# Local attention in a Trainium2 transformer block: query and key projections grouped ahead of each window's heads, one norm chain for both, and the softmax reciprocal taken before its broadcast

## The chip, the cores and the metric

One Trainium2 chip, all 8 cores; each core runs the same program on its own half of a sequence (4 sequences of 8192 tokens, 4096 tokens a core, with a halo of 1152 tokens recomputed). The metric is device microseconds of the slowest core.

## The reference

Two parts, each with a residual and a layer norm behind it. The first is a linear attention over the whole sequence. The second, `_L0_ffn_ref`, runs two layers, and the change lies in the attention of these two. Cut to what matters:

```python
def _layer(x, ...):                      # DEPTH = 2, HEADS = 8, DIM_HEAD = 64, WINDOW = 512
    h = shift_token(x)                   # upper half of the channels one token later
    q, k, v = jnp.split(h @ wqkv, 3, axis=-1)
    q = l2norm(q) * qs                   # t / max(norm(t), 1e-12), per head
    k = l2norm(k) * ksc
    q, k = rotary_xpos(q, k)
    o = local_attention(q, k, v)         # softmax over this window and the one before, masked
    x = x + o @ wo
    h = layernorm(shift_token(x)) @ w1 + b1
    a, g = jnp.split(h, 2, axis=-1)
    return x + (a * gelu(g)) @ w2 + b2
```

## The kernel before

The stages run one after another: a linear attention (`build_p1`, `build_p2`), then `build_layer(0)`, its MLP, `build_layer(1)`, its MLP, and a final norm. Every stage is written as a list of operations per engine; each engine runs its list in order, and an operation waits on semaphores for the operations named in its dependencies. So the order in which the operations are added is the order of each engine's queue.

The attention of `build_layer` goes over the sequence in windows of 512 tokens, `w` from 0 to 10. Four helpers do the projections of a window:

- `piece_tab` loads the rotary tables of one window by a DMA on the GpSimd queue, as soon as the last user of the tables is done.
- `piece_v` makes the values: 4 tiles of 128 tokens, 8 matmuls each into PSUM bank `P[6]`, and a copy to `vt` (line 943).
- `piece_q(pw, j)` makes the queries of one tile of 128 tokens: 8 matmuls into `P[2]` (line 959), Square on ScalarE (964), a sum per head on VectorE (966), Sqrt on ScalarE (970), max and reciprocal (972, 974), then the scaling that reads `P[2]` (976), the product with `qs_rep` (981) and three rotary operations (983, 987, 992).
- `piece_k(pw, j)` does the same for the keys in the same bank (lines 1004 to 1038). Its matmuls wait for the scaling of the queries at line 976, since that frees `P[2]`.
- `piece_T` transposes the rotated tiles on TensorE (1051, 1065) and copies them on ScalarE into `qf`, `kf_e`, `kf_o`. In the queues it stands ahead of `piece_q` of the next tile.

The attention for key window `pb = w - 1` loops over 8 heads. For each head and each of 4 key tiles, TensorE makes scores (line 1182, masks 1189 and 1193) into the banks 5/3 or 0/1 by turns, ScalarE exponentiates them (1196, 1200), and TensorE multiplies by the values (1138 into `P[6]` for the query window that ends here, called left, and 1145 into `P[7]` for the next one, called right). Line 1206 clears `P[7]` ahead of the second key tile and waits for the last copy out of it (1232). At the end of a head VectorE adds the saved half (1215), clamps the sum of weights (1217), and casts it (1219); TensorE broadcasts the sum over 64 partitions into `P[2]` (1221); VectorE takes the reciprocal of these 64x512 numbers (1225), multiplies (1227), and copies the right half to `O_acc` (1232). The first value product of the next head waits for 1227. After 8 heads the output projection follows (1264, 1268).

Windows 0 and 1 are projected in one piece ahead of the heads. From then on the projection of window `w + 1` is laid between the heads of window `w`: behind each even head one `piece_q`, behind each odd head one `piece_k`, and `piece_T` ahead of the following `piece_q`. The matmuls of `piece_q` and `piece_k` wait for line 1227, as the broadcast and the reciprocal use `P[2]` too. In iteration 9 of each layer there is nothing left to project, so its 8 heads run plain; iteration 10 has only the left half. In layer 1, iteration 1 has only the right half.

## Time and profile before

| | us |
|---|---|
| median of the runs | 11552.49 (2 runs, 11524.73 to 11580.26) |
| the profiled execution | 11389.46 |
| its span, first to last instruction of the slowest core | 11387.9 |
| TensorE busy | 6611.0 |
| VectorE busy | 3372.7 |
| ScalarE busy | 1937.8 |
| attention of layer 0 | about 2893 to 4949 |
| attention of layer 1 | about 7110 to 9094 |

The span runs from the first to the last instruction of the slowest core. A row of the trace gives the start, the duration, the engine, the line and the tiles, and in brackets how long the engine had been idle and what released it. A granted clock of 1.0 is TensorE's full speed, 0.5 the lower of its two levels.

### The profile page before, as it was taken

The page shows a single profiled execution, that of the slowest core. Times are in us where ns is not written, and L with a number is a line of the kernel's source. Part 1 is how long each engine was busy: PE and PEld are TensorE (multiplying, and loading weights), DVE is VectorE, ACT ScalarE, POOL GpSimd, SP SyncE. Part 2 cuts the span into 40 slices and gives each one's busy share as a digit, 9 for nine tenths or more (in the row PEclk, how much of TensorE's full clock was granted, in tenths as well). Part 3 has the DMA queues.
Part 4 walks back from the last instruction along what each step waited for, and adds up shares of the span by engine and source line. Part 5 has one row for each costly group of instructions (what it writes and reads, how often), then busy time and mean ns, then how long its engine had stood idle before and what let it go on. Part 6 is the DMA issues. An engine that isn't in the chain of part 4 may idle for free.

```text
span 11387.9 us, 75913 instructions; the slowest of 8 cores (11360.9 to 11387.9 us)
## 1 busy us (share of the span) xinstructions
PE 6611.0 (58%) x27498; PEld 2682.4 (24%) x27498; DVE 3372.7 (30%) x4692; ACT 1937.8 (17%) x3121; POOL 91.3 (1%) x136
## 2 busy tenths in 40 slices
PE   0488645554455555557687775555555567778821
PEld 0133211112122222223232222222222123222311
DVE  0011133333444444431212211344444410221234
ACT  0001011111132333210001000333233200101000
POOL 1000000000000000000000000000000000000000
PEclk9979877676666665656899987666665567989955
DMA  9501300000100000001122223000000001222221
GB/s 117 60 1 15 39 0 7 8 8 9 19 1 2 1 2 1 0 12 24 53 73 50 63 67 84 3 1 1 2 1 1 2 22 33 59 63 71 60 56 51
DMA packets 610316, 325.47 MB, mean 29 GB/s; under 512 B 489180, under 2 KB 541004, under 8 KB 608416
## 3 DMA queue, kind: packets, MB, share of 16 engines
q0 software_dynamic: 65024, 79.23, 5.7%
q1 hardware_dynamic: 310496, 137.55, 4.6%
q10 hardware_dynamic: 234432, 103.83, 3.6%
q8 instruction: 228, 3.74, 0.1%
q14 instruction: 136, 1.11, 0.0%
HBM read 374.31 MB, written 59.77 MB: 38 GB/s over the span
## 4 chain that ended last, share of the span: by engine, by line
PE 47%; DVE 22%; DMA 10%; ACT 8%; issue 7%; another core or an unknown queue 4%; DVEq 1%; ACTq 0%; POOL 0%; SPq 0%; POOLq 0%
PE M0b L1506 5%; PE M1b L1506 5%; DMA w2b<-w2bf 4%; DMA w1g<-w1bf 4%; PE kps L486 3%; PE vps L497 2%; DVE L0b L1225 2%; DVE L1b L1225 2%; PE M0b L1563 2%; ACT pt L1196 2%; PE p2b L747 2%; PE M1b L1563 2%; PE p2b L653 2%; PE p2b L632 2%
## 5 line engine op out<-in xcount | busy, mean ns | idle before, releaser
L1563 PE MATMUL M0b<-hbuf,w2b 128*128 128x512 bf16 (+1 forms) x1760 | 407.3, 384 | 167.6 <-DMA w2b<-w2bf 115.8
L1506 PE MATMUL M0b<-xt,w1a 128*128 128x512 bf16 (+1 forms) x1760 | 448.0, 403 | 89.2 <-DVE xt L1465 69.1
L486 PE MATMUL kps<-WkSb,X_g 128*128 128x512 bf16 x656 | 204.0, 468 | 426.1 <-DMA WvSb<-Wv 426.1
L1506 PE MATMUL M0b<-xt,w1g 128*128 128x512 bf16 (+1 forms) x1760 | 411.8, 379 | 60.4 <-DMA w1g<-w1bf 59.8
L1539 DVE SCALAR_TENSOR_TENSOR hbuf<-M0b,gout 128x512 bf16<-128x512 f32 x220 | 143.4, 652 | 1000.1 <-ACT gout L1531 988.6
L1506 PE MATMUL M1b<-xt,w1a 128*128 128x512 bf16 x1408 | 388.8, 426 | 76.7 <-DVE xt L1465 56.7
L1563 PE MATMUL M1b<-hbuf,w2b 128*128 128x512 bf16 x1408 | 345.1, 395 | 128.6 <-DMA w2b<-w2bf 86.1
L1539 DVE SCALAR_TENSOR_TENSOR hbuf<-M1b,gout 128x512 bf16<-128x512 f32 x176 | 121.8, 692 | 830.8 <-ACT gout L1531 821.7
L1506 PE MATMUL M1b<-xt,w1g 128*128 128x512 bf16 x1408 | 343.7, 388 | 17.3 <-DMA w1g<-w1bf 14.4
L1138 PE MATMUL L0b<-pt,vt 128*65 128x512 bf16 (+1 forms) x320 | 137.5, 430 | 314.9 <-ACT pt L1200 282.0
L1531 ACT ACTIVATE gout<-M0b 128x512 bf16<-128x512 f32 x220 | 124.4, 565 | 1096.4 <-PE M0b L1522 632.9
L1225 DVE RECIPROCAL L0b<-L0b 64x512 f32<-64x512 f32 x80 | 268.6, 3358 | 63.5 <-PE L0b L1221 63.5
L1138 PE MATMUL L1b<-pt,vt 128*65 128x512 bf16 (+3 forms) x288 | 122.7, 426 | 282.8 <-ACT pt L1200 249.1
L729 PE MATMUL p2tp<-ident_s,gated 128*128 128x128 bf16 x328 | 41.5, 306 | 407.0 <-DVE gated L718 407.0
L1531 ACT ACTIVATE gout<-M1b 128x512 bf16<-128x512 f32 x176 | 105.1, 597 | 935.6 <-PE M1b L1522 477.3
L1563 PEld LDWEIGHTS M0b<-hbuf,w2b 128*128 128x128 bf16 x1760 | 164.2, 104 | 409.9 <-issue 276.2
L632 PE MATMUL p2b<-X_g,WqSb 128*128 128x512 bf16 (+1 forms) x704 | 176.7, 423 | 143.0 <-DVE X_g L804 87.5
L1196 ACT ACT_TABLE_LOAD x130 | 166.8, 1283 | 540.6 <-PE L0b L1193 279.1
L1225 DVE RECIPROCAL L1b<-L1b 64x512 f32<-64x512 f32 x72 | 241.8, 3358 | 57.2 <-PE L1b L1221 57.2
L747 PE MATMUL p2b<-gatedT,WoSb 128*128 128x512 bf16 (+1 forms) x704 | 199.9, 440 | 83.1 <-ACT ao L751 69.3
L1196 ACT ACTIVATE pt<-L0b,mrowH 128x512 bf16<-128x512 f32 (+1 forms) x320 | 213.5, 670 | 198.0 <-PE L0b L1193 104.8
L1196 ACT ACTIVATE pt<-L1b,mrowH 128x512 bf16<-128x512 f32 (+1 forms) x320 | 213.4, 670 | 191.4 <-PE L1b L1193 98.5
(362 smaller groups left out, 10632.5 us busy)
## 6 DMA issues: line engine op xcount, KB each, us to landing
w1a<-w1bf SPq DMA_DIRECT2D x198, 256.0 KB, 3.3
w1g<-w1bf ACTq DMA_DIRECT2D x198, 256.0 KB, 3.4
w2b<-w2bf SPq DMA_DIRECT2D x198, 256.0 KB, 2.6
w2b<-w2bf ACTq DMA_DIRECT2D x198, 256.0 KB, 2.6
w1bf<-w POOLq DMA_DIRECT2D x8, 2816.0 KB, 210.4
outT<-fin_o SPq DMA_DIRECT2D x32, 512.0 KB, 3.5
w2bf<-w POOLq DMA_DIRECT2D x8, 1408.0 KB, 281.4
X_g<-x_extT POOLq DMA_DIRECT2D x4, 2624.0 KB, 43.9
```

The lines of the kernel that those rows point to most:

```text
L486: mm = s.add("tensor", lambda t, c=c, half=half, xs=xsl, st=(c == 0): t.matmul(kps[half][:, :], xs(c), Wk[:, c, 512 * half:512 * (half + 1 ...
L497: mm = s.add("tensor", lambda t, c=c, half=half, xs=xsl, st=(c == 0): t.matmul(vps[half][:, :], xs(c), Wv[:, c, 512 * half:512 * (half + 1 ...
L632: mm = s.add("tensor", lambda t, c=c, fin=fin, pb=pb, g0=g0, Ng=Ng, st=(fin == 0): t.matmul(P[pb][:, 0:Ng], Wq[:, fin, 128 * c:128 * (c + 1)],
L653: mm = s.add("tensor", lambda t, c=c, half=half, pb=pb, tcol=tcol, st=(c == 0): t.matmul(P[pb][:, :], sb["X"][:, c, tcol:tcol + 128], Wh[: ...
L747: mm = s.add("tensor", lambda t, c=c, fin=fin, pb=pb, Ng=Ng, st=(fin == 0): t.matmul(P[pb][:, 0:Ng], Wo[:, fin, 128 * c:128 * (c + 1)], ga ...
L1138: s.add("tensor", lambda t, j=j, h=h, kslot=kslot, n_l=n_l, st=st: t.matmul(P[6][0:65, 128 * j:128 * j + n_l], vt[kslot][:, j, 65 * h:65 * ...
L1196: e1 = s.add("scalar", lambda sc, j=j, kti=kti, qn=qn, bankF=bankF: sc.activation(pt[j % 2][:, 0:min(qn, 512)], bankF[:, 0:min(qn, 512)], ...
L1225: rcp = s.add("vector", lambda v: v.reciprocal(P[2][0:64, 0:512], P[2][0:64, 0:512]), [trp])
L1506: mm = s.add("tensor", lambda t, banks=banks, wt=wt, half=half, fin=fin, nn=nn, st=(fin == 0): t.matmul(banks[half][:, 0:nn], wt[:, fin, : ...
L1531: tg = s.add("scalar", lambda sc, jb=jb, half=half, nn=nn: sc.activation(gout[:, 512 * half:512 * half + nn], P[jb + 2 + half][:, 0:nn], A ...
L1539: th = s.add("vector", lambda v, j=j, jb=jb, half=half, nn=nn: v.scalar_tensor_tensor(h_buf[:, j, 512 * half:512 * half + nn], P[jb + half ...
L1563: mm = s.add("tensor", lambda t, c=c, j=j, sl=sl, half=half, nn=nn, st=(j == 0), sp=(j == 21): t.matmul(P[c][:, 0:nn], w2b[sl][:, 128 * c: ...
```

## The change

Four edits, all in `build_layer`. No projection is laid between heads any more: in every iteration with a window left, its values, queries, keys and transposes are done in one piece ahead of the heads. `piece_q` ends with a copy of the raw queries from PSUM to a bf16 tile, `qraw`, and the rest of its chain moves into `piece_k`, where one Sqrt, one max and one reciprocal serve both sums (16 numbers a token). And the reciprocal of the softmax sum is taken on one row of 512 numbers ahead of the cast and the broadcast, in place of on 64x512 behind it.

```diff
             def piece_q(pw, j):
...
                 t_qrd = rd
-                sq = s.add("scalar", lambda sc: sc.activation(
-                    bnf[:, 8:16], bnf[:, 0:8], AF.Sqrt), [rd])
...
-                t1 = s.add("vector", lambda v: v.tensor_tensor(
-                    ubuf[:, :], P[2][:, :],
-                    bass.AP(bnf, 8, [[24, 128], [1, 8], [0, 64]]),
-                    ALU.mult), [rc])
-                t_uq = t1
...
-                return s.add("vector", lambda v: v.tensor_add(
-                    qrot[:, :], qrot[:, :], ubuf[:, :]), [tb])
+                tqr = s.add("vector", lambda v: v.tensor_copy(
+                    qraw[:, :], P[2][:, :]), [rd])
+                t_uq = tqr
...
             def piece_k(pw, j):
...
-                    bnf[:, 16:24], xqk[:, :].rearrange("p (h d) -> p h d", d=64),
+                    bnf[:, 8:16], xqk[:, :].rearrange("p (h d) -> p h d", d=64),
                     AX.X, ALU.add), [tks])
                 sq = s.add("scalar", lambda sc: sc.activation(
-                    bnf[:, 16:24], bnf[:, 16:24], AF.Sqrt), [rd])
+                    bnf[:, 16:32], bnf[:, 0:16], AF.Sqrt), [rd])
...
+                t1 = s.add("vector", lambda v: v.tensor_tensor(
+                    ubuf[:, :], qraw[:, :],
+                    bass.AP(bnf, 16, [[32, 128], [1, 8], [0, 64]]),
+                    ALU.mult), [rc])
+                t2 = s.add("vector", lambda v: v.tensor_mul(
+                    qhat[:, :], ubuf[:, :], qs_rep[:, :]), [t1, t_w8])
...
+                tq = s.add("vector", lambda v: v.tensor_add(
+                    qrot[:, :], qrot[:, :], ubuf[:, :]), [tb])
                 t1 = s.add("vector", lambda v: v.tensor_tensor(
                     ubuf[:, :], P[2][:, :],
-                    bass.AP(bnf, 16, [[24, 128], [1, 8], [0, 64]]),
-                    ALU.mult), [rc])
+                    bass.AP(bnf, 24, [[32, 128], [1, 8], [0, 64]]),
+                    ALU.mult), [tq])
...
-                return tk
+                return tq, tk
...
-                if w < n_proj and w <= CL:
+                if w < n_proj:
                     piece_tab(w)
                     piece_v(w)
                     pend = None
                     for j in range(4):
                         if pend is not None:
                             piece_T(w, pend[0], pend[1], pend[2])
-                        tqt = piece_q(w, j)
-                        tkt = piece_k(w, j)
+                        piece_q(w, j)
+                        tqt, tkt = piece_k(w, j)
                         pend = (j, tqt, tkt)
                     piece_T(w, pend[0], pend[1], pend[2])
-                elif w < n_proj:
-                    piece_v(w)
...
+                            trc = s.add("vector", lambda v: v.reciprocal(
+                                tsum[64:65, :], tsum[64:65, :]), [tmx])
                             tcb = s.add("vector", lambda v: v.tensor_copy(
-                                rrowb[0:1, :], tsum[64:65, :]), [tmx])
+                                rrowb[0:1, :], tsum[64:65, :]), [trc])
                             trp = s.add("tensor", lambda t: t.matmul(
                                 P[2][0:64, 0:512], sb["ones_row"][0:1, 0:64], rrowb[0:1, :],
                                 start=True, stop=True), [tcb, t_tt1, t_uq, t_uk])
-                            rcp = s.add("vector", lambda v: v.reciprocal(
-                                P[2][0:64, 0:512], P[2][0:64, 0:512]), [trp])
                             to2 = s.add("vector", lambda v, h=h, B=B_left: v.tensor_tensor(
-                                tsum[0:64, :], P[2][0:64, :], ALU.mult), [rcp, t_wo2])
+                                tsum[0:64, :], P[2][0:64, :], ALU.mult), [trp, t_wo2])
...
-                        if il:
-                            ph = h
-                            jj = ph // 2
-                            if ph % 2 == 0:
...
-                                self._tq_il = piece_q(pw, jj)
-                            else:
-                                tkt = piece_k(pw, jj)
-                                pend_il = (jj, self._tq_il, tkt)
-                    if il:
-                        piece_T(pw, pend_il[0], pend_il[1], pend_il[2])
```

## Rows read from the trace of the kernel before

**Rows 1.** The page, busy time, share of the span and instructions by engine.
```profile
PE 6611.0 (58%) x27498; PEld 2682.4 (24%) x27498; DVE 3372.7 (30%) x4692; ACT 1937.8 (17%) x3121; POOL 91.3 (1%) x136
```

**Rows 2.** Windows: stretch, length, busy by engine, granted clock, DMA share, GB/s.
```profile
2976.05:3251.07 275.02, 143.56 (x488) 61.12 (x488) 122.05 (x189) 79.70 (x136) 1.48 (x2) 0.64 0.02 2
3251.07:4705.66 1454.59, 775.71 (x2744) 323.51 (x2744) 631.29 (x870) 466.49 (x756) 4.44 (x6) 0.61 0.01 1
4705.66:4853.48 147.82, 74.27 (x300) 31.87 (x300) 58.75 (x61) 36.74 (x69) 0.00 (x0) 0.60 0.00 0
2984.55:3064.26 79.71, 37.90 (x125) 16.70 (x123) 34.12 (x68) 18.38 (x37) 0.74 (x1) 0.68 0.03 4
4714.16:4723.35 9.19, 4.07 (x30) 2.12 (x29) 2.21 (x4) 5.29 (x9) 0.00 (x0) 0.99 0.01 2
7197.42:7396.85 199.43, 113.41 (x416) 52.81 (x416) 72.10 (x141) 79.69 (x136) 1.48 (x2) 0.67 0.02 3
7274.40:7396.85 122.45, 75.56 (x296) 36.30 (x296) 37.41 (x73) 66.71 (x108) 0.74 (x1) 0.62 0.03 4
7396.85:8851.94 1455.09, 777.10 (x2744) 324.28 (x2744) 631.30 (x869) 466.81 (x756) 4.45 (x6) 0.61 0.01 1
8851.94:8998.80 146.86, 73.07 (x300) 31.11 (x300) 58.94 (x62) 36.74 (x69) 0.00 (x0) 0.64 0.00 0
```

**Rows 3.** Groups by line on ScalarE: the table loads.
```profile
L1196 ACT ACT_TABLE_LOAD x130 | 166.8, 1283 | 540.6 <-PE L0b L1193 279.1 <-PE L1b L1193 259.5
L970 ACT ACT_TABLE_LOAD x65 | 83.4, 1283 | 57.3 <-DVE bnf L966 57.3
L1016 ACT ACT_TABLE_LOAD x64 | 82.1, 1283 | 55.7 <-DVE bnf L1012 55.7
```

**Rows 4.** Timeline, projections of window 0, layer 0 (start, us, engine, line, operation).
```profile
2904.44 1.89 PE L939 MATMUL L0b<-wqkv_l,X_g 128*128 128x512 bf16 x8 [0.95 <-DVE vt L943]
...
2942.64 0.69 DVE L966 TENSOR_REDUCE bnf<-xqk 128x8 f32<-128x512 bf16 x1 [5.23 <-ACT xqk L964]
...
2944.31 0.69 DVE L976 TENSOR_TENSOR ubuf<-L0b,bnf 128x512 bf16<-128x512 f32 x1
2945.10 0.42 DVE L981 TENSOR_TENSOR qhat<-ubuf,qsr 128x512 bf16<-128x512 bf16 x1
2945.15 3.39 PE L1004 MATMUL L0b<-wqkv_l,X_g 128*128 128x512 bf16 x8 [3.31 <-DVE ubuf L976]
...
2947.03 0.69 DVE L992 TENSOR_TENSOR qrot<-qrot,ubuf 128x512 f32<-128x512 f32 x1
...
2959.68 0.69 DVE L966 TENSOR_REDUCE bnf<-xqk 128x8 f32<-128x512 bf16 x1 [5.26 <-ACT xqk L964]
```

**Rows 5.** Timeline, one plain head of iteration 9, layer 0.
```profile
4805.44 0.69 DVE L1215 TENSOR_TENSOR tsum<-L0b,Oacc 65x512 f32<-65x512 f32 x1 [6.74 <-PE L0b L1145]
...
4807.31 0.60 PE L1221 MATMUL L0b<-rrowb,ones_row_g 1*64 1x512 bf16 x1 [2.05 <-DVE rrowb L1219]
...
4808.02 3.36 DVE L1225 RECIPROCAL L0b<-L0b 64x512 f32<-64x512 f32 x1 [0.85 <-PE L0b L1221]
...
4809.65 0.37 ACT L1200 ACTIVATE pt<-L0b,mrowH 128x128 bf16<-128x128 f32 x1
4811.48 0.68 DVE L1227 TENSOR_TENSOR osb<-tsum,L0b 64x512 bf16<-64x512 f32 x1
4812.26 0.69 DVE L1232 CAST Oacc<-L0b 65x512 bf16<-65x512 f32 x1
...
4813.10 0.60 PE L1206 MATMUL L0b<-zrow_g,ones_row_g 1*65 1x512 bf16 x1 [4.32 <-DVE Oacc L1232]
...
4814.35 0.63 PE L1138 MATMUL L0b<-pt,vt 128*65 128x512 bf16 x1
...
4819.69 0.69 DVE L1215 TENSOR_TENSOR tsum<-L0b,Oacc 65x512 f32<-65x512 f32 x1 [6.74 <-PE L0b L1145]
```

**Rows 6.** One line's instructions: the reciprocal of the earlier stage, min/median/max ns.
```profile
L786 DVE RECIPROCAL rowB<-rowB x11: 941/3341/3341, 1507.9 to 2837.0; 1x512 f32<-1x512 f32 x10, 1x128 f32<-1x128 f32 x1
```

More of the change, by code:

```diff
@@ L851, in build_layer @@
             xqk = self.sbuf(f"xqk{l}", (128, 512), BF16, es)
-            bnf = self.sbuf(f"bnf{l}", (128, 24), F32, es)
+            qraw = self.sbuf(f"qraw{l}", (128, 512), BF16, es)
+            bnf = self.sbuf(f"bnf{l}", (128, 32), F32, es)
             P = [self.psum(f"L{l}b{i}", (128, 512), F32, es) for i in range(8)]
@@ L969, in piece_q @@
                 t_qrd = rd
-                sq = s.add("scalar", lambda sc: sc.activation(
-                    bnf[:, 8:16], bnf[:, 0:8], AF.Sqrt), [rd])
-                mx = s.add("vector", lambda v: v.tensor_scalar(
-                    bnf[:, 8:16], bnf[:, 8:16], 1e-12, None, ALU.max), [sq])
-                rc = s.add("vector", lambda v: v.reciprocal(
-                    bnf[:, 8:16], bnf[:, 8:16]), [mx])
-                t1 = s.add("vector", lambda v: v.tensor_tensor(
-                    ubuf[:, :], P[2][:, :],
-                    bass.AP(bnf, 8, [[24, 128], [1, 8], [0, 64]]),
-                    ALU.mult), [rc])
-                t_uq = t1
-                t2 = s.add("vector", lambda v: v.tensor_mul(
-                    qhat[:, :], ubuf[:, :], qs_rep[:, :]), [t1, t_w8])
-                ta = s.add("vector", lambda v, j=j: v.tensor_tensor(
-                    ubuf[:, :], qhat[:, :],
-                    bass.AP(tabs, 256 * j + 0 * DF, [[4 * 4 * DF, 128], [0, 8], [1, DF]]),
-                    ALU.mult), [t2, t_tab])
-                tb = s.add("vector", lambda v, j=j: v.tensor_tensor(
-                    qrot[:, :].rearrange("p (h t x) -> p h t x", h=8, t=2),
-                    bass.AP(qhat, 32, [[512, 128], [64, 8], [-32, 2], [1, 32]]),
-                    bass.AP(tabs, 256 * j + 1 * DF, [[4 * 4 * DF, 128], [0, 8], [32, 2], [1, 32]]),
-                    ALU.mult), [ta, self.t_ttq])
-                return s.add("vector", lambda v: v.tensor_add(
-                    qrot[:, :], qrot[:, :], ubuf[:, :]), [tb])
+                tqr = s.add("vector", lambda v: v.tensor_copy(
+                    qraw[:, :], P[2][:, :]), [rd])
+                t_uq = tqr
             def piece_k(pw, j):
@@ L1016, in piece_k @@
                 sq = s.add("scalar", lambda sc: sc.activation(
-                    bnf[:, 16:24], bnf[:, 16:24], AF.Sqrt), [rd])
+                    bnf[:, 16:32], bnf[:, 0:16], AF.Sqrt), [rd])
                 mx = s.add("vector", lambda v: v.tensor_scalar(
-                    bnf[:, 16:24], bnf[:, 16:24], 1e-12, None, ALU.max), [sq])
+                    bnf[:, 16:32], bnf[:, 16:32], 1e-12, None, ALU.max), [sq])
                 rc = s.add("vector", lambda v: v.reciprocal(
-                    bnf[:, 16:24], bnf[:, 16:24]), [mx])
+                    bnf[:, 16:32], bnf[:, 16:32]), [mx])
+                t1 = s.add("vector", lambda v: v.tensor_tensor(
[4 more added lines that the diff above has]
+                    qhat[:, :], ubuf[:, :], qs_rep[:, :]), [t1, t_w8])
+                ta = s.add("vector", lambda v, j=j: v.tensor_tensor(
+                    ubuf[:, :], qhat[:, :],
+                    bass.AP(tabs, 256 * j + 0 * DF, [[4 * 4 * DF, 128], [0, 8], [1, DF]]),
+                    ALU.mult), [t2, t_tab])
+                tb = s.add("vector", lambda v, j=j: v.tensor_tensor(
+                    qrot[:, :].rearrange("p (h t x) -> p h t x", h=8, t=2),
+                    bass.AP(qhat, 32, [[512, 128], [64, 8], [-32, 2], [1, 32]]),
+                    bass.AP(tabs, 256 * j + 1 * DF, [[4 * 4 * DF, 128], [0, 8], [32, 2], [1, 32]]),
+                    ALU.mult), [ta, self.t_ttq])
+                tq = s.add("vector", lambda v: v.tensor_add(
+                    qrot[:, :], qrot[:, :], ubuf[:, :]), [tb])
                 t1 = s.add("vector", lambda v: v.tensor_tensor(
                     ubuf[:, :], P[2][:, :],
-                    bass.AP(bnf, 16, [[24, 128], [1, 8], [0, 64]]),
-                    ALU.mult), [rc])
+                    bass.AP(bnf, 24, [[32, 128], [1, 8], [0, 64]]),
+                    ALU.mult), [tq])
                 t_uk = t1
```

9 lines of the change are left out of this document (removed).

## The prediction

> **What bounds the kernel now.** I read the page first. TensorE is busy 58% of the span, VectorE 30%, ScalarE 17% [rows 1]: no engine is the bound, so a sum of busy times says little and chains of waits decide. The change touches only the attention of the two layers, so I cut that stage into its iterations, from the first value copy of one window to that of the next, with the windows view [rows 2], and read the timeline of one tile of projections [rows 4] and of one plain head [rows 5].
>
> The three kinds of work that the new kernel is built from all exist in this trace. Iterations 2 to 8 of layer 0, heads with projections laid between them, take 1454.59 us, so 207.8 each; layer 1 the same, 1455.09 or 207.9 [rows 2]. Iteration 9, with values, 8 plain heads and the output projection, takes 147.8 in layer 0 and 146.9 in layer 1 [rows 2] (its end is put where the next window's first value copy would have come, after the output projection). And windows 0 and 1 show a projection in one piece. Laying the projections between the heads so costs 207.8 - 147.8 = 60 us a window; in one piece they will have to cost less than that to gain.
>
> **Part 1: projections in one piece.** From the last value copy of iteration 1 to the first reciprocal of its heads there are 79.71 us; in iteration 9, without projections, the same distance is 9.19 [rows 2]. So the old form in one piece costs 79.7 - 9.2 = 70.5 us, more than the 60 it costs between the heads. The reason is in the timeline: a tile pair goes round in 2959.68 - 2942.64 = 17.04 us [rows 4], four make 68.2, and nothing else runs in it, whereas between heads the vector chain of a projection lies beside the scores and exponentials of the next head.
>
> **Part 2: the joined norm chain.** Removed from the way to the keys' matmuls: from the start of the queries' sum to the start of those matmuls there are 2945.15 - 2942.64 = 2.51 us [rows 4]. New: the sum 0.69 and 0.10 of spacing, the copy from PSUM, for which I take 0.69 like every 128x512 operation that reads PSUM here, and 0.15 to TensorE: 1.63. Saved 0.88. But the five query operations, which today run while TensorE makes the keys, now stand between the joint reciprocal and the scaling of the keys, on VectorE, and the keys' transposes and the next tile's matmuls wait behind them. From the start of the queries' scaling to the start of its last add there are 2947.03 - 2944.31 = 2.72 us, with 0.69 + 0.10 for the add itself: 3.51 [rows 4]. The scaling now reads bf16 from SBUF and f32 norms. Bounds are 0.69, as from PSUM, and 0.42, as the all-bf16 product behind it [rows 4]; one operand stays f32, so I take 0.69; the other end would give back 0.27. Sqrt, max and reciprocal of 16 numbers in place of 8 cost nothing visible, and the second set that is saved lay on the part already counted. Net per pair: 3.51 - 0.88 = +2.63, so 19.7 us, and +10.5 for four. The queries' transposes stay hidden: they are ready 3.5 us ahead of the keys'. In windows 0 and 1 this is a plain loss.
>
> **Part 3: table loads.** There are 130 + 65 + 64 = 259 loads of 1.283 us in the attention [rows 3]. After it there are one for Sqrt and one for Exp per window, 36 in all (windows 1 to 9 need one for Exp; 0 and 2 to 9 one for Sqrt): 223 fewer, 286 us of ScalarE. This is no term of its own: the plain head already has none of them, and 147.8 holds its one Exp load. The Sqrt load at a window's start lies on the chain: +1.3 for windows 2 to 9.
>
> The Trainium skill, "ScalarE: Activation LUTs", section "Table sets: the hidden batching unit", says to group activations by table set, which is what this change does and speaks for a gain; it prices a switch at about 2.7 us. The trace shows 1.283 for the load. What the rule would do here is the third rival below.
>
> **Part 4: the reciprocal ahead of the broadcast.** The one-row form exists in the trace: 3.341 us for 1x512 [rows 6], against 3.36 for 64x512 [rows 5]. So it costs the same; only its place changes. Today it runs behind the broadcast, and TensorE makes the next head's first scores beside it; afterwards TensorE waits for it. The head's chain is sum (4805.44), clamp, cast, broadcast (4807.31), reciprocal (4808.02), product (4811.48), copy (4812.26), clear of the bank (4813.10), and 6.59 us more to the next head's sum [rows 5]: 14.25. With the reciprocal ahead, each link stays, so the clear stands 7.66 us behind the sum as before. The first scores and their exponential now start behind the later broadcast. Today the last exponential of them ends 4809.65 + 0.37 - 4807.31 = 2.71 us behind the broadcast, and the first value product stands 4814.35 - 4813.10 = 1.25 behind the clear [rows 5]. In the new order the clear comes 0.71 + 0.68 + 0.10 + 0.84 = 2.33 behind the broadcast, the value product 3.58: it is later than 2.71 by 0.87. So a plain head still takes 14.25, and the cover that was lost was not needed. Only in iteration 10, without copy and clear, the value product could start 1.5 behind the broadcast and must wait for the exponential: 0 to 1.2 a head, taken as 0.6, for 16 heads 10 us, 5 a layer. The table DMA of each window is issued during the heads before and costs nothing; uncovered it would delay the first rotary product.
>
> **The sum, layer 0.** Inserting projections costs 70.5 + 10.5 = 81.0, with a Sqrt load 82.3. Window 0: +10.5. Iteration 1: 147.8 + 81.0 - 275.0 = -46.2, as the projection of window 2 leaves it. Iterations 2 to 8: 7 x (147.8 + 82.3) - 1454.6 = +156.1. Iteration 9: +82.3. Iteration 10: +5. Total +208.
>
> **Layer 1.** Window 0: +10.5. Iteration 1 has no left half, so a plain head there needs the 6.59 and 0.84 from copy to clear, 7.43; eight and some 4 us around them are 63.5 in place of 122.45 [rows 2]: -59.0, with the pairs -48.5. Iterations 2 to 8: 7 x (146.9 + 82.3) - 1455.1 = +149.3. Iteration 9 +82.3, iteration 10 +5. Total +199.
>
> Together +406 us. On the profiled execution, 11389.5, that is 11796; on the median of the runs, 163 us higher for reasons that its profile can't show, 11959, or 3.5% more. The predicted time goes by the median, rounded to 11950.
>
> **The rivals.**
>
> *The clock rises.* The clock in the projections is 0.68 and in the plain windows 0.60 to 0.64 [rows 2]; eight matmuls take 3.39 us where they take 1.89 at full clock [rows 4]. In the new order TensorE's idle time inside a tile pair shrinks between queries and keys (3.31 to about 2.4) and a head's matmuls stand closer together. If the keys' matmuls ran at full clock, 80 x 1.50 = 120 us come back; for the heads, the two plain windows differ by 0.96 us for 0.04 of clock, so some 9 us a window up to full clock, 18 windows: 165. Then +406 - 285 = +121, 11673 by the median: within 2%. Against it: TensorE's wait behind the key matmuls grows by the 3.5 us of the query chain, and the one in front of the broadcast from 2.05 to 5.4 [rows 5], and the key matmuls behind 3.31 us of idle time are slow today [rows 4]. The Trainium skill, "TensorE: Matmul & The Clock Gate", section "Loop structure matters more than you think", warns that waits between bursts of matmuls drop the clock; the trace agrees in those rows, and the rule speaks against this change. Chance 12%.
>
> *The lost cover matters.* If the next head's first scores and exponential came out exposed behind the later broadcast, up to 2.2 us a head (2.71 less the 0.5 of the broadcast itself) for 144 heads would add 317: 12276. The margin is 0.87 us, so this decides once they take 0.9 us longer than now. Chance 5%.
>
> *The table loads were the price.* If the laying-between cost only its loads, and all else stayed hidden as now, 286 us would come back: 11266, faster by 2.5%. It decides if the one-piece projection takes under about 60 - 286 / 16 = 42 us a window. The 70.5 us of the serial form speak against it: the vector chain and not the load fills them. Chance 3%.
>
> **How the numbers follow.** My forecast has 80%, and the range of 8 in 10 is its own: 11740 (half of the clock's 285 us comes back and the median falls by half of its 163 us towards the profiled execution) to 12070 (the sum by the median with 110 us of exposed chain or of slower matmuls). The clock's rival in full lies below it, the lost cover in full above, and so does the loads' rival, below. About 2% is what a measurement tells from no change here. Slower by over 2%: forecast and lost cover, 85%, of which one is moved to within 2% for a clock between the two, so 84%. Within 2%: 13%. Faster: 3%.
>
> **What the profile of the changed kernel would show.** Value copies of iterations 2 to 9 about 230 us apart. A tile pair every 19.7 us. Plain heads every 13.7 to 14.3 us, with TensorE idle 5.4 in front of the broadcast. A one-row reciprocal of 3.34. 36 table loads in the attention. The MLP unchanged. The prediction is wrong if pairs take under 17 us, heads under 12 or over 15, or if the MLP's clock moves with the attention's.

## The result

The changed kernel is slower. Its median is 11940.5 us (11743.6 to 12076.3, 11 runs) against 11534.5 us of the kernel before (11353.6 to 11628.2, 10 runs). The medians count all runs; the ratio, 1.0323 with a 95% interval of 1.0218 to 1.0428, is taken over the fast ones alone, those in which no die ran longer than the other at a lower clock. The forecast was 11950. One execution was profiled; it took 11837.0 us on its slowest core, and its span is 11835.4.

Nearly all the time went where the argument put it, into the attention: 392 us, where the medians are 406 apart. I measure a layer's attention from the first to the last instruction that uses its PSUM banks, and take the median of the eight cores of the one profiled execution:

| us | before | after | difference |
|---|---|---|---|
| attention, layer 0 | 2072.0 | 2275.4 | +203.4 |
| attention, layer 1 | 1999.8 | 2188.6 | +188.8 |
| both | 4071.8 | 4464.0 | +392.2 |
| both MLPs | 3925.9 | 3926.5 | +0.6 |

The predicted +406 stands against +392. The same two stages are the measure of all the experiments below.

The page of the changed kernel, busy time by engine. Against [rows 1] ScalarE has lost 288 us, nearly all of it loads, and the span has grown all the same.

```profile
PE 6689.1 (57%) x27498; PEld 2689.5 (23%) x27498; DVE 3400.4 (29%) x4612; ACT 1649.9 (14%) x2817; POOL 91.5 (1%) x136
```

The windows view of the changed kernel: stretch, length, busy time of TensorE, its weight loads, VectorE, ScalarE and GpSimd, granted clock, DMA share, GB/s. The first two rows are the two attentions of this core, the next two iteration 1 and iterations 2 to 7 of layer 0, then the same of layer 1, and last the MLP of layer 1.

```profile
2821.22:5092.26 2271.04, 1076.10 (x3792) 445.59 (x3792) 929.51 (x1214) 473.54 (x867) 6.69 (x9) 0.60 0.01 1
7236.40:9429.78 2193.38, 1055.02 (x3720) 440.03 (x3720) 879.70 (x1166) 474.44 (x868) 6.70 (x9) 0.59 0.01 1
2929.37:3154.72 225.35, 107.20 (x392) 45.23 (x392) 91.51 (x120) 47.55 (x89) 0.74 (x1) 0.62 0.01 1
3154.72:4529.38 1374.66, 659.35 (x2352) 275.82 (x2352) 549.39 (x722) 292.79 (x540) 4.45 (x6) 0.60 0.01 2
7348.27:7496.05 147.78, 84.57 (x320) 38.67 (x320) 41.66 (x73) 46.78 (x89) 0.74 (x1) 0.57 0.02 2
7496.05:8871.91 1375.86, 662.34 (x2352) 276.61 (x2352) 549.38 (x722) 293.01 (x540) 4.45 (x6) 0.59 0.01 2
9430.00:11328.07 1898.07, 1457.09 (x5520) 533.77 (x5520) 328.01 (x412) 142.51 (x198) 1.06 (x2) 0.76 0.19 49
```

Six iterations take 1374.66 us in layer 0, 229.1 each, and 1375.86 or 229.3 in layer 1, where before took 207.8 and 207.9 [rows 2]. Iteration 1 shows both signs at once: in layer 0 it fell from 275.02 to 225.35, since the projection of window 2 has moved out of it into iteration 2. That time comes back at the other end: iteration 9, which had no projection before, now has one. The last row is a warning about reading a single execution: MLP 1 takes 1898.07 us at a granted clock of 0.76 here, and 1785.56 at 0.85 in the profile of before. Only cores 4 and 5 show it; the six others take 1789 to 1819, and the median of the MLPs has not moved.

The groups by line on ScalarE, the table loads of the changed attention (sum of us, mean ns, idle time before them): 35 in place of the 259 of [rows 3].

```profile
L1186 ACT ACT_TABLE_LOAD x18 | 23.1, 1283 | 20.3 <-PE L0b L1183 10.2 <-PE L1b L1183 10.2
L996 ACT ACT_TABLE_LOAD x17 | 21.8, 1283 | 14.7 <-DVE bnf L992 14.7
```

The timeline of the changed kernel, one tile pair of projections and one plain head (start, us, engine, line, operation, idle time before it and what ended that), which answer to [rows 4] and [rows 5].

```profile
4090.41 0.69 DVE L1002 TENSOR_TENSOR ubuf<-qraw,bnf 128x512 bf16<-128x512 bf16 x1
...
4093.92 0.69 DVE L1019 TENSOR_TENSOR ubuf<-L0b,bnf 128x512 bf16<-128x512 f32 x1
...
4104.45 3.11 PE L984 MATMUL L0b<-wqkv_l,X_g 128*128 128x512 bf16 x8 [2.42 <-DVE qraw L971]
...
4110.15 0.69 DVE L1002 TENSOR_TENSOR ubuf<-qraw,bnf 128x512 bf16<-128x512 bf16 x1
...
4237.01 0.69 DVE L1205 TENSOR_TENSOR tsum<-L0b,Oacc 65x512 f32<-65x512 f32 x1 [6.25 <-PE L0b L1135]
...
4238.32 3.35 DVE L1209 RECIPROCAL tsum<-tsum 1x512 f32<-1x512 f32 x1
...
4242.33 0.60 PE L1213 MATMUL L0b<-rrowb,ones_row_g 1*64 1x512 bf16 x1 [5.50 <-DVE rrowb L1211]
...
4244.66 0.60 PE L1196 MATMUL L0b<-zrow_g,ones_row_g 1*65 1x512 bf16 x1 [0.87 <-DVE Oacc L1222]
...
4244.67 0.37 ACT L1190 ACTIVATE pt<-L0b,mrowH 128x128 bf16<-128x128 f32 x1
...
4245.92 0.63 PE L1128 MATMUL L0b<-pt,vt 128*65 128x512 bf16 x1
...
4250.71 0.69 DVE L1205 TENSOR_TENSOR tsum<-L0b,Oacc 65x512 f32<-65x512 f32 x1 [6.20 <-PE L0b L1135]
```

A pair goes round in 4110.15 - 4090.41 = 19.74 us, where before took 17.04 [rows 4]. The queries' five operations stand where the forecast put them: the keys' scaling starts at 4093.92, 3.51 behind the queries'. In the head, the reciprocal now ends before the broadcast, TensorE waits 5.50 us for it where it waited 2.05 [rows 5], and yet the period is 4250.71 - 4237.01 = 13.70, no longer than before.

### The profile page after: what moved, and what is told of

Same layout as the page of the kernel before. It is cut to its first block, busy times and chain, and to the rows that moved or that the text cites. A ratio compares the mean times of both kernels' runs of the same rounds, so it can differ in the third digit from the quotient of the medians.

```text
span 11835.4 us, 75712 instructions; the slowest of 8 cores (11752.8 to 11835.4 us)
## 1 busy us (share of the span) xinstructions
PE 6689.1 (57%) x27498; PEld 2689.5 (23%) x27498; DVE 3400.4 (29%) x4612; ACT 1649.9 (14%) x2817; POOL 91.5 (1%) x136
## 4 chain that ended last, share of the span: by engine, by line
PE 48%; DVE 26%; DMA 9%; issue 6%; ACT 6%; another core or an unknown queue 4%; DVEq 1%; ACTq 0%; POOL 0%; SPq 0%; POOLq 0%
PE M1b L1482 6%; PE M0b L1482 6%; DVE tsum L1209 4%; DMA w2b<-w2bf 4%; DMA w1g<-w1bf 3%; PE kps L486 3%; PE vps L497 2%; PE M0b L1539 2%; PE M1b L1539 2%; PE p2b L747 2%; PE p2b L653 2%; PE p2b L632 1%; PE L0b L1240 1%; PE L1b L1240 1%
## 5 line engine op out<-in xcount | busy, mean ns | idle before, releaser
L1209 DVE RECIPROCAL tsum<-tsum 1x512 f32<-1x512 f32 x152 | 508.3, 3344 | 16.0 <-DVE tsum L1207 0.5
L1482 PE MATMUL M1b<-xt,w1a 128*128 128x512 bf16 x1408 | 434.6, 465 | 77.0 <-DVE xt L1441 56.6
L1539 PE MATMUL M1b<-hbuf,w2b 128*128 128x512 bf16 x1408 | 390.1, 436 | 112.7 <-DMA w2b<-w2bf 71.4
L1482 PE MATMUL M1b<-xt,w1g 128*128 128x512 bf16 x1408 | 376.0, 416 | 8.5 <-DMA w1g<-w1bf 8.2
L1213 PE MATMUL L0b<-rrowb,ones_row_g 1*64 1x512 bf16 x80 | 48.0, 600 | 440.7 <-DVE rrowb L1211 440.7
L1213 PE MATMUL L1b<-rrowb,ones_row_g 1*64 1x512 bf16 x72 | 43.2, 600 | 396.7 <-DVE rrowb L1211 396.7
L1482 PEld LDWEIGHTS M0b<-xt,w1a 128*128 128x128 bf16 x1760 | 160.5, 104 | 322.9 <-issue 206.7
```

Of the source, the lines that this page charges most:

```text
L1209: trc = s.add("vector", lambda v: v.reciprocal(tsum[64:65, :], tsum[64:65, :]), [tmx])
L1482: mm = s.add("tensor", lambda t, banks=banks, wt=wt, half=half, fin=fin, nn=nn, st=(fin == 0): t.matmul(banks[half][:, 0:nn], wt[:, fin, : ...
L1539: mm = s.add("tensor", lambda t, c=c, j=j, sl=sl, half=half, nn=nn, st=(j == 0), sp=(j == 21): t.matmul(P[c][:, 0:nn], w2b[sl][:, 128 * c: ...
```

## The experiments

My theory: laying the projections between the heads was cheap because the vector chain lay beside other work; done in one piece it stands alone, and the joined chain makes the piece longer, since the queries' operations now stand in front of the keys'. The rivals: one piece alone is no loss worth the name, or all of it; the lost cover of the reciprocal costs time; the table loads were the real price. The first three kernels each take one edit of the change alone, on the kernel before, and the fourth one that is not in the change; the next two start from the changed kernel, and the last two put together what was gained. All attention times below are those of one profiled execution each.

**Placement alone.** The projections go in one piece; the two chains and the reciprocal stay as in before.

```diff
-                if w < n_proj and w <= CL:
+                if w < n_proj:
...
-                elif w < n_proj:
-                    piece_v(w)
...
-                    il = (CL < pw < n_proj)
+                    il = False
```

> Only the first edit: all projections in one piece ahead of the heads, with the old norm chains and the old reciprocal. The two attention stages take 2072 + 2000 = 4072 us before and 2271 + 2193 = 4464 after. Theory A (the loss has two parts: projections that no longer lie beside the heads' work, and the queries' rotary chain that came onto the path): this edit alone gives 16 windows about +11 us each and the small corrections of the first iterations, +186 in the two stages, tile pairs every 17.0 us, plain heads every 13.7 to 14.3 us; about 1.6% in the total. Rival B (the placement is the whole loss, and the joined chain costs nothing): +390 here.

Measured: attention 2173.1 + 2100.3 = 4273.4, +201.6. The ratio is 1.0118 (1.0076 to 1.016). So placement carries half of the loss. A pair took 17.66 us on the mean of 60: the first of a window, with the Sqrt load in it, 18.43, and the others 17.28, near the 17.04 of [rows 4]. This kernel has the loads nearly all taken away too, 18 + 17 are left, and loses all the same.

**The joined chain alone.** `piece_q` and `piece_k` as in the change, but called between the heads as before.

```diff
-                                self._tq_il = piece_q(pw, jj)
+                                piece_q(pw, jj)
                             else:
-                                tkt = piece_k(pw, jj)
-                                pend_il = (jj, self._tq_il, tkt)
+                                tqt, tkt = piece_k(pw, jj)
+                                pend_il = (jj, tqt, tkt)
```

> Only the second edit: queries and keys share Sqrt, maximum and reciprocal, and the raw queries are copied out of PSUM, but the projections stay laid between the heads. Theory A: behind a head with a query projection the exponentials no longer queue behind a reduction, two table loads and a Sqrt on ScalarE, so these head periods fall from 20.8 to about 17.1 us; the periods with a key projection stay near 21, since VectorE has some 3 us to spare before the next head's sum; windows 0 and 1 lose 10.5 us each in both layers; together about -190 us in the two attention stages (1.6% faster). Rival B: the five query operations that moved behind the keys fill VectorE in front of the head's sum, the key periods grow by 3.5 us, and the sum is within 20 us of no change.

Measured: 1970.8 + 1893.2 = 3864.0, -207.8; the ratio is 0.98 (0.9749 to 0.9852). The same edit that makes the changed kernel slower makes this one faster. The timeline of this kernel, one head with queries beside it and one with keys:

```profile
3076.15 0.60 ACT L965 ACTIVATE xqk<-L0b 128x512 bf16<-128x512 f32 x1 [3.77 <-PE L0b L960]
...
3076.90 0.69 ACT L1193 ACTIVATE pt<-L0b,mrowH 128x512 bf16<-128x512 f32 x1 [0.15 <-PE L0b L1190]
...
3084.56 3.36 DVE L1222 RECIPROCAL L0b<-L0b 64x512 f32<-64x512 f32 x1 [0.85 <-PE L0b L1218]
...
3102.38 0.69 DVE L1035 TENSOR_TENSOR krot<-krot,ubuf 128x512 f32<-128x512 f32 x1
...
3102.99 0.68 DVE L1212 TENSOR_TENSOR tsum<-L0b,Oacc 65x512 f32<-65x512 f32 x1
...
3105.56 3.36 DVE L1222 RECIPROCAL L0b<-L0b 64x512 f32<-64x512 f32 x1 [0.85 <-PE L0b L1218]
```

Behind the squares of the queries the exponential starts at once (3076.90): no load, no Sqrt. A head with queries then takes 16.36 us on the mean (15.5 to 17.2), where it took 20.8 before. A head with keys takes 21.0 (3105.56 - 3084.56): it has both loads, and VectorE works through both chains, so that the last add of the keys (3102.38) ends just as the next head's sum starts (3102.99). Four heads with queries save 17.9 us a window; the heads with keys give back 0.7 of it, and the stretch from one window's last head to the next one's first, 64.15 us for 62.14, another 2.0. That is some 15 us for each of 16 windows, 243; windows 0 and 1 of both layers, in one piece, give back 42 at the forecast's 10.5 a window, which leaves 201.

**The reciprocal first, alone.**

```diff
+                            trc = s.add("vector", lambda v: v.reciprocal(
+                                tsum[64:65, :], tsum[64:65, :]), [tmx])
                             tcb = s.add("vector", lambda v: v.tensor_copy(
-                                rrowb[0:1, :], tsum[64:65, :]), [tmx])
+                                rrowb[0:1, :], tsum[64:65, :]), [trc])
...
-                            rcp = s.add("vector", lambda v: v.reciprocal(
-                                P[2][0:64, 0:512], P[2][0:64, 0:512]), [trp])
```

> Only the last edit: the reciprocal on one row ahead of the cast and the broadcast. Theory A (it only changes place in an unbroken chain): head periods as before, 20.6 to 21.1 with projections between and 13.7 to 14.3 plain, iteration 10 from 9.4 to 10.1 us a head, so about +12 us in the two attention stages. Rival (TensorE now stands idle through it, so the next head's scores come late or its clock falls): plain heads over 15 us, or over +60 in the stages.

Measured, in a single run: 2114.3 + 2034.3 = 4148.6, +76.8. This is a miss: the rival's bound of +60 was passed, but with the plain heads unchanged, so not for its reason. The place is plain in the timeline. First the kernel before, a head between projections:

```profile
3104.89 0.37 PE L1221 MATMUL L0b<-rrowb,ones_row_g 1*64 1x512 bf16 x1 [1.98 <-DVE rrowb L1219]
3105.19 1.11 PE L1051 MATMUL L0b<-identF_g,qrot 128*128 128x128 f32 x4
3107.11 1.09 PE L1065 MATMUL L0b<-identF_g,krot 128*128 128x128 f32 x4 [0.82 <-ACT qf L1055]
3109.65 3.57 PE L959 MATMUL L0b<-wqkv_l,X_g 128*128 128x512 bf16 x8 [1.45 <-DVE osb L1227]
```

Then the same head with the reciprocal first:

```profile
3090.96 0.60 PE L1223 MATMUL L0b<-rrowb,ones_row_g 1*64 1x512 bf16 x1 [5.43 <-DVE rrowb L1221]
3091.49 1.12 PE L1051 MATMUL L0b<-identF_g,qrot 128*128 128x128 f32 x4
3093.43 1.09 PE L1065 MATMUL L0b<-identF_g,krot 128*128 128x128 f32 x4 [0.82 <-ACT qf L1055]
3094.31 3.62 PE L959 MATMUL L0b<-wqkv_l,X_g 128*128 128x512 bf16 x8
```

In before, the transposes of the previous tile lie beside the reciprocal of 3.36 us, and the next queries start 3109.65 - 3104.89 = 4.76 behind the broadcast, waiting for the product alone. With the reciprocal first, the broadcast comes 5.43 - 1.98 = 3.45 later, and the queries stand 3.35 behind it, because now the transposes hold them up: 3.45 + 3.35 - 4.76 = +2.04. The heads that carry transposes went from 20.8 to 22.8 us on the mean; there are three of them a window in 16 windows, 48 x 2.0 = 96. The 16 heads of iteration 10 add 12, and the stretch from one window's heads to the next's got 2.3 us shorter (59.80 for 62.14), which gives 16 x 2.3 = 37 back: 71 in all. The plain heads of iteration 9 didn't move, as forecast. So the reciprocal did cover something, only not in the plain heads where I had looked.

**The norm without Sqrt, in place.** Before, with the norm's factor as exp(-0.5 ln(max(sum, 1e-24))) in both chains in place of Sqrt, max and reciprocal. Nothing is moved.

```diff
-                sq = s.add("scalar", lambda sc: sc.activation(
-                    bnf[:, 8:16], bnf[:, 0:8], AF.Sqrt), [rd])
                 mx = s.add("vector", lambda v: v.tensor_scalar(
-                    bnf[:, 8:16], bnf[:, 8:16], 1e-12, None, ALU.max), [sq])
-                rc = s.add("vector", lambda v: v.reciprocal(
-                    bnf[:, 8:16], bnf[:, 8:16]), [mx])
+                    bnf[:, 8:16], bnf[:, 0:8], 1e-24, None, ALU.max), [rd])
+                sq = s.add("scalar", lambda sc: sc.activation(
+                    bnf[:, 8:16], bnf[:, 8:16], AF.Ln), [mx])
+                rc = s.add("scalar", lambda sc: sc.activation(
+                    bnf[:, 8:16], bnf[:, 8:16], AF.Exp, scale=-0.5), [sq])
```

> The kernel before, with 1/norm made as exp(-0.5 ln(max(sum, 1e-24))) on ScalarE, in place of Sqrt, maximum and reciprocal, so that the table set need not change between the heads if one set serves both functions. If the 256 loads between heads vanish: theory A, whose price for laying projections between heads is the reduction, the two loads and the Sqrt that the next head's exponentials queue behind, expects 2.6 us off each of 128 head periods less 0.3 for the second function: 20.8 to about 18.4, some -290 us in the two attention stages. Rival (the loads lie beside other work): under -60 us. If the loads stay, the run only shows one more short function per chain, about +30 us.

Measured: 1917.2 + 1830.2 = 3747.4, -324.4; the ratio is 0.9688 (0.961 to 0.9766). ScalarE's queue between two heads in the kernel before:

```profile
3113.32 0.60 ACT L964 ACTIVATE xqk<-L0b 128x512 bf16<-128x512 f32 x1 [3.78 <-PE L0b L959]
3114.78 1.28 ACT L970 ACT_TABLE_LOAD   x1 [0.87 <-DVE bnf L966]
3116.08 0.21 ACT L970 ACTIVATE bnf<-bnf 128x8 f32<-128x8 f32 x1
3116.30 1.28 ACT L1196 ACT_TABLE_LOAD   x1
3117.60 0.69 ACT L1196 ACTIVATE pt<-L0b,mrowH 128x512 bf16<-128x512 f32 x1
```

and in this kernel:

```profile
3082.88 0.60 ACT L964 ACTIVATE xqk<-L0b 128x512 bf16<-128x512 f32 x1 [3.90 <-PE L0b L959]
3084.92 0.21 ACT L972 ACTIVATE bnf<-bnf 128x8 f32<-128x8 f32 x1 [1.44 <-DVE bnf L970]
3085.22 0.21 ACT L974 ACTIVATE bnf<-bnf 128x8 f32<-128x8 f32 x1
3085.33 0.67 ACT L1196 ACTIVATE pt<-L0b,mrowH 128x512 bf16<-128x512 f32 x1
```

From the squares to the head's first exponential there are 3117.60 - 3113.32 = 4.28 us before and 3085.33 - 3082.88 = 2.45 here. Both loads of each projection are gone, two are left in the attention of both layers, and a head between projections takes 18.5 us on the mean (17.5 to 19.2) in place of 20.8. The 257 loads that went have 257 x 1.283 = 330 us, and 324 us came back. The edit also moved the reciprocal of the norm from VectorE to ScalarE, but that is 0.20 us against 0.21: the loads lay on the path, nearly all of them. The Trainium skill, "ScalarE: Activation LUTs", section "Table sets: the hidden batching unit", names one set that holds both Exp and Ln; the trace agrees, with 2 loads left of 259.

**The changed kernel with the old reciprocal.** `trc` goes out and `rcp` back behind the broadcast; the other edits stay.

```diff
-                            trc = s.add("vector", lambda v: v.reciprocal(
-                                tsum[64:65, :], tsum[64:65, :]), [tmx])
...
+                            rcp = s.add("vector", lambda v: v.reciprocal(
+                                P[2][0:64, 0:512], P[2][0:64, 0:512]), [trp])
```

> The changed kernel with the reciprocal back behind the broadcast, on 64x512. The changed kernel takes 4464 us in the two attention stages. The same edit made in the kernel before cost +77 there, because the reciprocal had covered the transposes of the projection. Theory A: with no projection between the heads there is nothing but the next head's first scores to cover, which has room, so here it is worth only iteration 10, 16 heads at 10.15 in place of 9.4 us: -12 us. Rival C (the cost is the longer idle time in front of the broadcast and comes anywhere): -60 us or more.

Measured, in a single run: 2270.6 + 2188.6 = 4459.2, 4.8 less than the changed kernel, which is within what its cores differ by (2263.3 to 2274.2 in layer 0). A plain head takes 13.87 on the mean against 13.92, a head of iteration 10 9.44 against 10.20. With the first two experiments this splits the +392.2 along a chain of kernels: placement +201.6, the joined chain on top of it +185.8, the reciprocal on top of both +4.8.

**The changed kernel with the transposes later.** In one piece, tile j's query matmuls now go ahead of the transposes of tile j - 1; they wait for `t_uk`, the last reader of their bank, as well.

```diff
                     for j in range(4):
+                        piece_q(w, j)
                         if pend is not None:
                             piece_T(w, pend[0], pend[1], pend[2])
-                        piece_q(w, j)
                         tqt, tkt = piece_k(w, j)
```

> The changed kernel with the transposes of tile j-1 placed between the query and the key matmuls of tile j, in place of ahead of both; the query matmuls then wait for the keys' scaling, the last reader of their bank. Theory A (the tile pair is one chain, and the keys' product, rotary operations and transposes lie on it only through TensorE's order): the 3.8 us between the end of that scaling and the next query matmuls shrink to 0.15, so pairs fall from 19.5 to about 16, for 60 pairs some -205 us in the two attention stages. Rival D (VectorE's own queue, which still has the keys' four operations in front of the next sum, or the transposes in front of the key matmuls, sets the pair): under -60 us.

Measured: 2149.7 + 2053.9 = 4203.6, 260.4 less than the changed kernel, by moving one line. Against before the ratio is 1.0106 (1.0068 to 1.0143): it gives back two thirds of the loss. The timeline of a tile pair:

```profile
2938.89 0.69 DVE L1019 TENSOR_TENSOR ubuf<-L0b,bnf 128x512 bf16<-128x512 f32 x1
...
2939.73 3.27 PE L960 MATMUL L0b<-wqkv_l,X_g 128*128 128x512 bf16 x8 [6.94 <-DVE ubuf L1019]
...
2942.84 0.60 PE L1048 MATMUL L0b<-identF_g,qrot 128*128 128x128 f32 x4
...
2944.32 0.63 PE L1062 MATMUL L0b<-identF_g,krot 128*128 128x128 f32 x4 [0.88 <-ACT qf L1052]
...
2945.42 1.89 PE L984 MATMUL L0b<-wqkv_l,X_g 128*128 128x512 bf16 x8 [0.48 <-DVE qraw L971]
```

The next queries' matmuls wait for the keys' scaling and no longer for the keys' rotation, addition and transposes. The transposes fall into the gap before the key matmuls; TensorE's idle time there shrinks from 2.42 us to 0.48, and in this pair those eight matmuls take 1.89 us, at a granted clock of 1.00, where they took 3.11 at 0.58. That is not so in every pair: of the 60 groups with transposes in front 36 take 1.89, the others 3.04 to 3.48. The rows of the key matmuls of layer 0 in the kernel with placement alone (core 3, as records are missing on its slowest), the changed kernel and this one (sum of us for 40 groups, mean ns of one matmul, idle time before them):

```profile
L1004 PE MATMUL L0b<-wqkv_l,X_g 128*128 128x512 bf16 x320 | 136.3, 604 | 143.2 <-DVE ubuf L976 143.2
L984 PE MATMUL L0b<-wqkv_l,X_g 128*128 128x512 bf16 x320 | 117.8, 534 | 96.9 <-DVE qraw L971 96.9
L984 PE MATMUL L0b<-wqkv_l,X_g 128*128 128x512 bf16 x320 | 106.7, 494 | 31.8 <-DVE qraw L971 31.8
```

Over both layers a group takes 3.41, 2.94 and 2.59 us, so the faster matmuls give 80 x 0.35 = 28 of this kernel's 260 us. Pairs take 15.9 us on the mean (14.5 to 17.8) in place of 19.8. So what made the piece of the changed kernel dear was mostly the order in which TensorE waited for the vector chain, not the amount of work in it. But the piece in its best order is still the dearer place: this kernel's attention is 131.8 us longer than before.

**What was gained, put together.** The joined chain between the heads, Ln and Exp for its norm, and the later transposes in windows 0 and 1.

```diff
-                    bnf[:, 16:32], bnf[:, 0:16], AF.Sqrt), [rd])
+                    bnf[:, 16:32], bnf[:, 16:32], AF.Ln), [mx])
+                rc = s.add("scalar", lambda sc: sc.activation(
+                    bnf[:, 16:32], bnf[:, 16:32], AF.Exp, scale=-0.5), [sq])
...
+                        piece_q(w, j)
                         if pend is not None:
                             piece_T(w, pend[0], pend[1], pend[2])
-                        piece_q(w, j)
```

> The kernel before with projections laid between the heads, plus the joined chain of the change, the ln and exp form of the norm, and the later transposes in windows 0 and 1. Theory A: what each gave alone adds up as far as it takes away the same queue in front of the exponentials: periods with a query projection 16.2, with a key projection about 18.8, so pairs of heads 35.0 in place of 41.6 before, 37.1 with ln and exp alone and 37.3 with the joined chain alone; about -440 us in the two attention stages (to 3630), 3.8% faster than before. Rival E: with both, VectorE's 3.5 us of query operations no longer fit in front of the next head's sum in the shorter key period, which stays at 20 or more: -330 or less.

Measured: 1890.8 + 1805.0 = 3695.8, -376.0 to before; the ratio is 0.9667 (0.9588 to 0.9746). That is 64 us less gain than I had expected. Heads with queries take 16.2 us on the mean (15.6 to 16.9), as forecast, heads with keys 19.6 (19.1 to 20.1) where 18.8 was forecast, and the timeline shows why:

```profile
3206.36 3.36 DVE L1222 RECIPROCAL L0b<-L0b 64x512 f32<-64x512 f32 x1 [0.62 <-PE L0b L1218]
...
3210.66 3.41 PE L984 MATMUL L0b<-wqkv_l,X_g 128*128 128x512 bf16 x8 [4.40 <-DVE osb L1224]
...
3214.22 0.60 ACT L989 ACTIVATE xqk<-L0b 128x512 bf16<-128x512 f32 x1 [10.89 <-PE L0b L984]
```

The key matmuls wait 4.40 us for the product behind the reciprocal, since broadcast and projection share a bank. So all that comes behind the keys starts late: VectorE gets the squares' sum only then, and both chains of the pair run into the next head's sum.

**A bank of its own for the broadcast.** The last kernel with broadcast, reciprocal and product in `P[4]`, which the transposes use, so that the projection's matmuls need not wait for the product. The transposes wait for it instead, and stand behind the query matmuls.

```diff
-                        deps = [t_uk, t_uq, t_tt1]
+                        deps = [t_uk, t_uq]
...
-                                P[2][0:64, 0:512], sb["ones_row"][0:1, 0:64], rrowb[0:1, :],
+                                P[4][0:64, 0:512], sb["ones_row"][0:1, 0:64], rrowb[0:1, :],
...
                             if ph % 2 == 0:
+                                piece_q(pw, jj)
                                 if pend_il is not None:
                                     piece_T(pw, pend_il[0], pend_il[1], pend_il[2])
                                     pend_il = None
-                                piece_q(pw, jj)
```

> The same with the broadcast and the reciprocal in the transposes' bank, so that the projection's matmuls no longer wait for the head's reciprocal and product, and with the transposes behind the query matmuls. Theory A (the reciprocal stands in the chain of the projection's bank): the matmuls, 3.4 us, run beside the reciprocal, and periods without transposes fall by about 2.8 us; those with transposes, which now wait for the product, fall by about 1: some -230 us against the run before it in the two attention stages. Rival F: Square, sum and norm still stand in front of the exponentials in ScalarE's queue and the sum now waits for the reciprocal on VectorE, so nothing is gained: within 40 us.

Measured: 1769.0 + 1709.7 = 3478.7, 217.1 less than the kernel before it and 593 less than before. The median is 10848.0 us, the ratio 0.9476 (0.9417 to 0.9535): faster than both kernels of this case. Its timeline, the start of the keys and the end of that head:

```profile
3300.17 0.60 PE L1218 MATMUL L0b<-rrowb,ones_row_g 1*64 1x512 bf16 x1 [1.98 <-DVE rrowb L1216]
...
3300.70 3.59 PE L984 MATMUL L0b<-wqkv_l,X_g 128*128 128x512 bf16 x8
...
3300.88 3.36 DVE L1222 RECIPROCAL L0b<-L0b 64x512 f32<-64x512 f32 x1 [0.85 <-PE L0b L1218]
...
3313.50 0.69 DVE L1035 TENSOR_TENSOR krot<-krot,ubuf 128x512 f32<-128x512 f32 x1
...
3314.11 0.68 DVE L1212 TENSOR_TENSOR tsum<-L0b,Oacc 65x512 f32<-65x512 f32 x1
```

The key matmuls start 0.53 us behind the broadcast and run beside the reciprocal. A head with keys takes 15.9 us on the mean (15.6 to 16.2) in place of 19.6, and the first of a window, with queries and nothing to transpose, 13.2 (12.4 to 14.3) in place of 16.2. A head with queries and transposes takes 17.0 (16.6 to 17.8) in place of 16.3: it was to fall by 1 us and rose by 0.75, since its transposes now wait for the product. So the total came out near its forecast, -217 for -230, by two misses that offset each other: the key heads fell by 3.7 and not by 2.8. The keys' last add (3313.50) still ends as the next sum starts (3314.11), so VectorE's order may be the next thing in the way of a head with keys; no run tries it.

## Why the prediction was right

The step that decided was **part 1**, the comparison of two figures that were both in the trace: 60 us for laying a projection between heads and 70.5 for one in one piece. Placement alone came out at +201.6 where I had expected +186: the decision and its size held. It holds even for the piece in its best order, which still costs +131.8.

**Part 2** was mis-sized by little. The pair was forecast at 19.7 and is 19.83 on the mean of 60 (18.1 to 21.8); that the two agree so well is luck in part, as the pair that it started from was put 0.6 too low and what was added to it 0.46 too high. The 3.51 us between the two scalings, and the 0.69 for the scaling from `qraw`, came out as taken. But on top of the one-piece kernel the joined chain cost +185.8, where 2.63 x 4 x 20 windows make 210: the pairs that it replaced took 17.66 on the mean and not 17.04, so that 2.17 a pair was added, and 2.17 x 80 = 174 (counted from the keys' sums, 17.20 and 19.88, it was 2.68). What the part left out is the key matmuls: it took them as unchanged, and eight of them fell from 3.41 us to 2.94, by 0.47, the size of what is missing between 2.63 and 2.17. What the part did not tell is that 2.63 is the price of one order of TensorE's queue. With the next queries ahead of the transposes the pair falls to 15.9, below that of before.

**Part 3** held: 35 loads against 36 forecast, and apart from the 1.3 for the Sqrt load at each window's start the loads were no term of the sum. That the old price of the laying-between held its loads in full was not seen: -324.4 without them in place. The third rival was right that the loads were a price (they cost 324 us, more than the 286 it had) and wrong that this change could collect it. A table load taken away between heads shortens the path; the same load taken away by moving the projection out is paid for by the chain that then stands alone.

**Part 4** held for the kernel it was made for. The last exponential ends 4244.67 + 0.37 - 4242.33 = 2.71 behind the broadcast and the value product starts 4245.92 - 4242.33 = 3.59 behind it, so 0.88 against the 0.87 forecast. Plain heads take 13.9 us in both kernels. A head of iteration 10 grew from 9.45 to 10.20, by 0.75 and not 0.6, 12 us for 16 heads against 10 in the sum; in all, the edit costs 4.8. The text said that the cover was not needed; that is so only because edit 1 had taken the transposes away from behind the broadcast. In the old placement the cover was needed, and the edit alone costs 76.8.

**The sum.** By stage, +203.4 and +188.8 stand against +208 and +199. By edit, +201.6, +185.8 and +4.8 stand against +186, +210 and +10, so the total is closer than its parts: an excess of 16 and shortfalls of 24 and 5 offset each other. Iterations 2 to 7 take 229.1 and 229.3 us against 230.1 and 229.2; iteration 1 takes 225.35 against 147.8 + 81.0 = 228.8, and in layer 1 147.78 against 150.9, because a head without a left half takes 6.93 and not 7.43. The step from the profiled execution to the median was the weaker one: 163 us were added for what the profile can't show, and the profiled execution of the changed kernel took 11837.0 where the sum said 11796. Of those 41, -14 are the attention, +112 MLP 1 on the slowest core, and -56 lie ahead of the attention, which starts at 2821 and not at 2877: two differences between executions, the first of them on two cores only and the second ahead of everything that was changed, which happened to offset each other in part. That 11950 lies 10 us from the median is therefore luck; what the argument can claim is the size of the loss, 392 in the stages for a forecast of 406.

**The rivals.** Over the two attentions the clock did not rise: 0.60 and 0.59, against 0.62 and 0.61 before. But in the key matmuls, where this rival put its first term, it did in part: they took 2.94 us a group against 3.41 with placement alone, behind 2.42 us of idle time and not 3.31, so 80 x 0.47 = 38 of its 120 us came back. The heads gave nothing back: plain ones kept their 13.9 us. With the transposes moved into the gap another 28 us came, and that kernel's total of +132, near the +121 worked out for this rival, is chance: most of its 260 us are a wait that went, not a faster clock. The lost cover decided nothing in this kernel (13.9 and 13.9).

**What stays open.** Why the medians of the kernel before differ between chips and sets of runs (11534, 11429, 11436) was not tried; the ratios of the experiments are against runs of the kernel before on the same chip. The last two kernels were not taken apart further: the joining of the chain is not priced separately from the Ln and Exp, and in the last one the new bank not from the transposes behind the query matmuls. Why the key matmuls run faster in some pairs than in others was not tried either.

## What to carry to other kernels

Before grouping work to save set-up costs, price both places from the trace: what the piece costs between the other work, and what it costs standing alone, where its serial chain is all there is. A small edit has no price of its own: the joined chain is worth -208 us between heads and +186 in one piece, and the reciprocal first +77 and +5, so measure or forecast each edit in the placement that it will have. And in an in-order queue ask of each wait whether anything behind it could go first: one call moved ahead of the transposes was worth 260 us, and a bank of its own for the broadcast, together with such a move, 217.

## What the runs showed of the hardware

- Ln and Exp ran with no load between them: with the norm from Ln and Exp, 2 loads were left in the attention of both layers in place of 259.
- A reciprocal of one row took as long as one of 64: 3.35 us for 1x512 and 3.36 for 64x512, both f32. Taking it on the row saves nothing, which made its place all there was to choose.
- Eight matmuls of 128x512 right behind 2.42 us of TensorE idle time took 1.89 to 3.57 us in the changed kernel, 2.94 on the mean of 80 groups, and 3.41 behind 3.31 us and more in the kernel with placement alone. With the transposes in the gap, 36 of 60 groups took 1.89 us at a granted clock of 1.00, behind 0.11 to 0.48 us; the other 24 had no idle time at all right in front and took 3.04 to 3.48 at 0.54 to 0.62. So the idle time just in front of a group does not decide its clock alone.
